# Turning P in one go: regrouped turns, copies and output projection in a fused attention and feed-forward kernel

## The chip, the cores and the metric

One core of a Trainium2 chip runs the whole program. The metric is the device time of one execution in microseconds. The engines are TensorE (PE, with PEld for its weight loads), VectorE (DVE), ScalarE (ACT), GpSimd (POOL) and SyncE (SP), which issues the transfers. Each runs its own queue in the order written and waits on semaphores.

## The reference

The input is 8 sequences of 256 tokens with 128 features. A first, small attention block of 8 heads comes ahead of the part that matters here. Then come 6 layers (DEPTH), each of them applied to the 8 sequences:

```python
def attn_layer(x, Wqkv, qs, ksc, Wo):          # 16 heads of 64, windows of 32 tokens
    q, k, v = split(x @ Wqkv, 3)
    q, k = l2norm(q) * qs, l2norm(k) * ksc     # then rotary tables on both
    out = local_attention(q, k, v)             # 32 queries see 64 keys (own and former window), softmax
    return out @ Wo                            # 1024 -> 128

def ffn_layer(x, g, bln, W1, b1, W2, b2):
    xn = (x - mean(x)) / sqrt(var(x) + 1e-05) * g + bln
    a, gate = split(xn @ W1 + b1, 2)           # 2 x 341
    return a * gelu(gate, approximate=False) @ W2 + b2

for i in range(DEPTH):
    x = attn_layer(shift_tokens(x), ...) + x
    x = ffn_layer(shift_tokens(x), ...) + x
```

## The kernel before

The 6 layers times 8 sequences are 48 units, numbered g (a "pair" in the code, since each has two halves of 128 tokens, m = 0 and 1; n = 2 * pair + m counts the halves). There is one pass, called slot, for each. Every engine has a function of the name slot(g) in its own queue, which lists the steps in an order written out by hand; all are tied by semaphores only. The slots 0 to 2 are written out, 3 to 46 are a hardware loop on TensorE and VectorE, and slot 47 is written out again. The pass works on four things at once: the attention of sequence g; the projections of q, k and v for g + 1; the output projection, residual and norm of g - 1; and the feed-forward part of f = g - 3 (LAG is 3).

A half of the attention goes like this. TensorE computes the scores of the 16 heads in two groups (g = 0 and 1 in those functions, a count of heads here, not of the pass). VectorE takes the maximum and subtracts it (centre, L1370 and L1374), into s_sb. ScalarE applies the exponential in place (exps, L1060). TensorE turns the probabilities P by transposes of 64x128 blocks into PSUM banks 4 and 5 (turn_p, which uses turn, L684), ScalarE copies them to p_t (copy_p, L1066), and TensorE multiplies them with V (attend, L766). VectorE normalises the result (L1382, L1385), TensorE turns it (turn_o), ScalarE copies it to o_t (copy_o, L1075), and in the next pass project_out (L788) multiplies it with wo_sb into bank 0.

In turn_p the first group of 8 transposes waits for both centrings and for its exponential. The second group waits for its own exponential and for the first copy, because both groups use the same places of banks 4 and 5. In between TensorE has other work: in the first half of a pass the second half of project_out(g - 1), in the second half of a pass the down projection of the feed-forward part (down, L834).

The order of the steps around this, in the first half of the pass on TensorE: scores, q of g + 1, gates_up (L806 to L808), project_out part 0, k of g + 1 (L671 to L675), turn_p 0, project_out part 1, turn_p 1, values_up (L806 to L808), attend, turn_k and turn_q, v, turn_o. In the second half: scores, q, k, turn_p 0, down, turn_p 1, mean (L795), attend, turn_k and turn_q of g + 1, variance (L801), v, turn_o.

These waits matter. The k step waits for the first gate activation (bank 7). values_up waits for all three gate activations, and its third tile, which goes to bank 0, waits for att_done (L826):

```python
up(ps[:, 1, 0:N], 0, 0)
up(ps[:, 1, N:2 * N], 0, 1).then_inc(s["f_value_up"], 1)
pe.wait_ge(s["att_done"], CREDIT + (f + LAG ...))
up(ps[:, 0, 0:N], 0, 2).then_inc(s["f_value_up"], 1)
```

att_done is given by VectorE's residual (L1393), which waits for project_out. On VectorE the first half of a pass is centre 0 and 1, the rotation products for q (L1345, L1349) and for k (L1345, L1349, which wait for k of g + 1), residual, products of the feed-forward part (L1411), normalise 0 and 1, norms (L1359). The second half has the same with add (L1418) and subtract_mean (L1400) ahead of normalise. The variance on TensorE waits for all four normalisations of the pass, since it uses bank 2.

ScalarE runs in the first half: gates (a table load at L1104, three activations at L1111, a table load back at L1113), exps 0, copy_p 0, exps 1, high (the rounding of the next input, L1011 and L1012), copy_p 1, the squares of q and k (L1019), and then the copies of k, q, o and v. In one pass of each layer a weight of the next layer is rounded here (L939), and in another one twice in the second half. The gates wait for the layer's biases.

Of the kernel before, what the change touches and what calls it, by code (L numbers as in the profile page):

```python
# [35 lines left out]
H, D = 16, 64  # L36
INNER = H * D
W = 32
SPAN = 64
# [25 lines left out]
def build(nc, xT, w1s, w2s, w3T, woT, cT, wmod, wqkv, scales, wo, params, w1, w2, consts, out):  # L65
    with ExitStack() as ctx:
# [198 lines left out]
        def layer_of(f):  # L265
            return f >> 3
# [255 lines left out]
        def _(pe):  # L522
# [155 lines left out]
            def turn(bank, c, src):  # L678


                width = src.shape[1]
                for t in range(2):
                    r = slice(64 * t, 64 * t + 64)
                    mm = pe.transpose(ps[0:width, bank + t, 64 * c:64 * c + 64], src[r], ident[r, r],  # L684
                                      tile_position=(64 * t, 0))
                return mm
# [48 lines left out]
                                           tile_position=(D * c, W * w))  # L735
                mm.then_inc(s["scored"], 1)

            def turn_p(pair, m, g):
                n = 2 * pair + m
                if g == 0:  # L740
                    pe.wait_ge(s["centred"], CREDIT + 2 * n + 2)
                else:
                    pe.wait_ge(s["p_copied"], CREDIT + 2 * n + 1)
                pe.wait_ge(s["exped"], CREDIT + 2 * n + g + 1)
                pe.sem_inc(s["pe_waited"], 1)
                for hh in range(4):
                    mm = turn(4, hh, s_sb[:, g, 2 * hh:2 * hh + 2, :].rearrange("p c k -> p (c k)"))
                mm.then_inc(s["p_turned"], 1)

            def attend(pair, m, g, over_q=True):  # L750

                n = 2 * pair + m
                if g == 0:
                    pe.wait_ge(s["v_moved"], CREDIT + 16 * (18 * pair + 8 + 10 * m))
                    pe.wait_ge(s["p_copied"], CREDIT + 2 * n + 2)
                    pe.sem_inc(s["pe_waited"], 1)
                elif over_q:
                    pe.wait_ge(s["roped"], CREDIT + 4 * n + 10)
                    pe.wait_ge(s["squared"], CREDIT + 2 * n + 5)
                    pe.sem_inc(s["pe_waited"], 1)  # L760
                for hh in range(4):
                    for w in range(4):
                        for c in range(2):
                            r = slice(D * c, D * c + D)
                            h = 4 * g + hh
                            mm = pe.matmul(ps[W * w:W * w + W, 4 - 2 * g + c, ON * hh:ON * hh + ON],  # L766
                                           p_t[r, h, W * w:W * w + W], v_sb[r, m, w, VD * h:VD * h + ON],
                                           start=True, stop=True, skip_group_check=True,
                                           tile_position=(D * c, W * w))
                mm.then_inc(s["attended"], 1)  # L770
# [6 lines left out]
                    mm = turn(2, c, o_n[:, P * c:P * c + P])  # L777
                mm.then_inc(s["o_turned"], 1)

            def project_out(pair, half):  # L780

                if half == 0:
                    pe.wait_ge(s["o_copied"], CREDIT + 2 * pair + 2)
                    pe.wait_ge(s["w_a_loaded"], 16 * layer_of(pair) + 16)
                    pe.wait_ge(s["centred"], CREDIT + 4 * pair + 5 if not isinstance(pair, int) or pair < SLOTS - 1
                               else CREDIT + 4 * pair + 4)
                for c in range(4 * half, 4 * half + 4):
                    mm = pe.matmul(ps[:, 0, 0:N], wo_sb[:, c, :], o_t[:, c, :], start=(c == 0),  # L788
                                   stop=(c == H // 2 - 1), skip_group_check=True)
                if half:  # L790
                    mm.then_inc(s["projected"], 1)

            def mean(f):
                pe.wait_ge(s["f_shifted"], CREDIT + 2 * f + 2)
# [43 lines left out]
            def slot(g, out=True, ff=True, ahead=True):  # L838
                scores(g, 0, 0)
                scores(g, 0, 1)  # L840
                if ahead:
                    q(g + 1, 0)
                if ff:
                    gates_up(g - LAG)
                if out:
                    project_out(g - 1, 0)
                if ahead:
                    k(g + 1, 0, gates=ff)
                turn_p(g, 0, 0)
                if out:  # L850
                    project_out(g - 1, 1)
                turn_p(g, 0, 1)
                if ff:
                    values_up(g - LAG)
                attend(g, 0, 0)
                attend(g, 0, 1, over_q=ahead)
                turn_k(g, 1)
                turn_q(g, 1)
                if ahead:
                    v(g + 1, 0)  # L860
                turn_o(g, 0)

                scores(g, 1, 0)
                scores(g, 1, 1)
                if ahead:
                    q(g + 1, 1)
                    k(g + 1, 1)
                turn_p(g, 1, 0)
                if ff:
                    down(g - LAG)  # L870
                turn_p(g, 1, 1)
                if out:
                    mean(g - 1)
                attend(g, 1, 0)
                attend(g, 1, 1, over_q=ahead)
                if ahead:
                    turn_k(g + 1, 0)
                    turn_q(g + 1, 0)
                if out:
                    variance(g - 1)  # L880
                if ahead:
                    v(g + 1, 1)
                if out:
                    pe.wait_ge(s["f_log"], CREDIT + g)
                turn_o(g, 1)
# [27 lines left out]
                slot(pe.snap(g))  # L913
            slot(SLOTS - 1, ahead=False)
            pe.wait_ge(s["f_done"], CREDIT + SLOTS - LAG)
            project_out(SLOTS - 1, 0)
            project_out(SLOTS - 1, 1)
            pe.wait_ge(s["f_centred"], CREDIT + SLOTS - 1)
            mean(SLOTS - 1)
            variance(SLOTS - 1)  # L920
# [5 lines left out]
        def _(act):  # L926
# [132 lines left out]
                v = s_sb[:, g, :, :].rearrange("p h k -> p (h k)")  # L1059
                act.activation(v, v, ACT.Exp).then_inc(s["exped"], 1)  # L1060

            def copy_p(pair, m, g):
                n = 2 * pair + m
                act.wait_ge(s["p_turned"], CREDIT + 2 * n + g + 1)
                act.wait_ge(s["attended"], CREDIT + 2 * n)
                act.activation(p_t[:, 4 * g:4 * g + 4, :].rearrange("p c (t k) -> p t c k", t=2),  # L1066
                               pair_of_banks(2)[:, :, 0:4 * SPAN].rearrange("p t (c k) -> p t c k", c=4),
                               ACT.Copy)\
                   .then_inc(s["p_copied"], 1)

            def copy_o(pair, m):
# [42 lines left out]

            def slot(g, ff=True, norm=True, out=True, ahead=True, more=True, after=None, layer=None):

                if ff:
                    gates(g - LAG)
                exps(g, 0, 0)
                if after == 7:  # L1120
                    round_weights(layer, 2)
                copy_p(g, 0, 0)
                exps(g, 0, 1)
                if ahead:
                    high(g + 1, 1)
                copy_p(g, 0, 1)
                if ahead:
                    square_of(g + 1, 0, 0)
                    square_of(g + 1, 0, 1)
                copy_k(g, 1)  # L1130
                copy_q(g, 1)
                if out:
                    shift(g - 1)
                copy_o(g, 0)
                if ahead:
                    copy_v(g + 1, 0)
                    inverse_norms(g + 1, 0)

                exps(g, 1, 0)
                if norm:  # L1140
                    round_norm(g - 2)
                if after == 6:
                    round_weights(layer, 0)
                if after == 2:
                    round_up(layer)
                copy_p(g, 1, 0)
                exps(g, 1, 1)
                if more:
                    high(g + 2, 0)
                copy_p(g, 1, 1)  # L1150
                if after == 6:
                    round_weights(layer, 1)
                if ahead:
                    square_of(g + 1, 1, 0)
                if out:
                    square(g - 1)
                if ahead:
                    square_of(g + 1, 1, 1)
                    copy_k(g + 1, 0)
                if out:  # L1160
                    inverse_deviation(g - 1)
# [50 lines left out]
        def _(dve):  # L1212
# [151 lines left out]
            def centre(pair, m, g):  # L1364
# [5 lines left out]
                dve.tensor_reduce(mx, src, AX.X, ALU.max)\  # L1370
                   .then_inc(s["maxed"], 1)
                dve.wait_ge(s["maxed"], CREDIT + 2 * n + g + 1)
                dve.wait_ge(s["p_turned"], CREDIT + 2 * n)
                dve.tensor_tensor(s_sb[:, g, :, :].rearrange("p (h a) k -> p a h k", a=2), src,  # L1374
                                  mx.unsqueeze(3).to_broadcast([P, 2, 4, SPAN]), ALU.subtract).then_inc(s["centred"], 1)

# [187 lines left out]
```

## Time and profile before

| | us |
|---|---|
| median of 3 runs | 1783.48 |
| lowest and highest | 1780.46, 1783.8 |
| the profiled execution | 1771.68 |
| its span, first to last instruction | 1769.9 |

| engine | busy us | share of the span |
|---|---|---|
| TensorE matmuls | 1633.4 | 92% |
| TensorE weight loads | 1264.3 | 71% |
| VectorE | 1340.1 | 76% |
| ScalarE | 1292.9 | 73% |
| GpSimd | 1061.1 | 60% |

The profile is of one execution. Matmuls overlap and their ends are modelled, so that starts are more to be trusted than ends. In the timeline a row gives its start, its duration, engine, line and operation, what it writes and reads, how many instructions were merged into the row, and in brackets how long the engine stood idle before it and for whom.

### The profile page before, as it was taken

How to read it: one execution, taken by the hardware profiler on the slowest of the kernel's cores; microseconds unless marked ns; L12 is line 12 of the kernel's file. 1: busy time of each engine (PE TensorE's matmuls, PEld its weight loads, DVE VectorE, ACT ScalarE, POOL GpSimd, SP SyncE). 2: the span in 40 equal slices, each digit the busy share in tenths (PEclk: the TensorE clock that was granted, in tenths of full speed). 3: DMA queues.
4: the chain of work that ended last, by engine and by line, in shares of the span. 5: the costliest groups of instructions: out<-in, count | busy, mean ns of one | idle time of the engine just before them, and what ended most of it. 6: DMA issues, size and time to landing. Idle time of an engine off the chain costs nothing.

```text
span 1769.9 us, 88661 instructions
## 1 busy us (share of the span) xinstructions
PE 1633.4 (92%) x36636; PEld 1264.3 (71%) x36636; DVE 1340.1 (76%) x1952; ACT 1292.9 (73%) x2124; POOL 1061.1 (60%) x767
## 2 busy tenths in 40 slices
PE   4898677799999999999999999999999999999985
PEld 2466455677777777777777777777777777777764
DVE  4465666688888878888887888888887878888852
ACT  3687445677877778777788777878777787777763
POOL 4000345567866767867678766668676676767630
PEclk8899889999999999999999999999999999999997
DMA  2000142222242222333222422222422222222220
GB/s 95 1 1 0 25 116 59 52 70 66 67 128 59 67 59 69 103 88 74 53 69 59 128 66 71 69 52 65 122 69 71 66 67 70 70 67 69 66 47 25
DMA packets 75302, 116.88 MB, mean 66 GB/s; under 512 B 17246, under 2 KB 26716, under 8 KB 74332
## 3 DMA queue, kind: packets, MB, share of 16 engines
q1 hardware_dynamic: 75228, 115.99, 26.4%
q8 instruction: 35, 0.57, 0.1%
q14 instruction: 39, 0.32, 0.1%
HBM read 19.04 MB, written 1.05 MB: 11 GB/s over the span
## 4 chain that ended last, share of the span: by engine, by line
PE 87%; issue 6%; ACT 4%; DVE 3%; DMA 0%; POOL 0%; ACTq 0%; SPq 0%; DVEq 0%
PE ps L684 14%; PE ps L788 10%; PE ps L671 9%; PE ps L766 9%; PE ps L731 8%; PE ps L675 7%; PE ps L674 7%; PE ps L834 4%; PE ps L724 2%; PE ps L806 2%; PE ps L808 2%; PE ps L807 2%; PE ps L801 2%; PE ps L795 2%; PE ps L582 1%
## 5 line engine op out<-in xcount | busy, mean ns | idle before, releaser
L411 POOL TENSOR_TENSOR arena<-arena,rnorm 128x1024 f32<-128x1024 f32 x192 | 361.6, 1904 | 352.3 <-ACT rnorm L1030 352.3
L402 POOL TENSOR_TENSOR arena<-arena 128x1024 f32<-128x1024 f32 x192 | 456.6, 2378 | 18.5 <-DVE arena L1349 15.1
L684 PEld LDWEIGHTS ps<-cst,arena 64*128 64x128 f32 x6144 | 224.4, 140 | 127.8 <-issue 119.0
L1345 DVE TENSOR_TENSOR arena<-ps,rope 128x1024 f32<-128x1024 f32 x192 | 234.7, 1222 | 94.9 <-issue 82.1
L684 PE MATMUL ps<-cst,arena 64*128 64x64 f32 x6144 | 276.8, 231 | 17.0 <-ACT arena L1060 9.4
L1066 ACT ACTIVATE arena<-ps 128x512 f32<-128x512 f32 x192 | 114.6, 597 | 175.5 <-PE ps L684 175.2
L1349 DVE TENSOR_TENSOR arena<-ps,rope 128x1024 f32<-128x1024 f32 x192 | 233.2, 1215 | 0.0
L674 PE MATMUL ps<-wqkv_lo,x_hi 128*128 128x512 f32 x576 | 229.2, 398 | 1.1 <-issue 1.1
L675 PE MATMUL ps<-wqkv_hi,x_hi 128*128 128x512 f32 x576 | 230.1, 399 | 0.0
L671 PE MATMUL ps<-wqkv_hi,x_lo 128*128 128x512 f32 x576 | 216.2, 457 | 14.8 <-issue 12.9
L1359 DVE TENSOR_REDUCE norm<-arena 128x16 f32<-128x1024 f32 x192 | 224.3, 1209 | 0.0
L1370 DVE TENSOR_REDUCE rmax<-ps 128x8 f32<-128x512 f32 x192 | 131.8, 686 | 109.0 <-PE ps L731 108.5
L766 PE MATMUL ps<-v_sb,arena 64*32 64x66 f32 x12288 | 166.5, 226 | 35.4 <-issue 19.3
L1019 ACT ACTIVATE arena<-ps 128x1024 f32<-128x1024 f32 x192 | 190.3, 1020 | 11.1 <-DVE arena L1349 11.1
L766 PEld LDWEIGHTS ps<-v_sb,arena 64*32 64x32 f32 x12288 | 138.2, 106 | 73.1 <-issue 62.9
L788 PE MATMUL ps<-arena,wo_sb 128*128 128x256 f32 x768 | 188.5, 389 | 1.2 <-issue 1.2
L731 PE MATMUL ps<-k_t,arena 64*32 64x64 f32 x12288 | 166.6, 224 | 8.2 <-issue 8.2
L1046 ACT ACTIVATE k_t<-ps 128x1024 f32<-128x1024 f32 x96 | 98.4, 1025 | 82.0 <-PE ps L684 79.5
L731 PEld LDWEIGHTS ps<-k_t,arena 64*32 64x32 f32 x12288 | 134.6, 105 | 32.4 <-issue 9.3
L788 PEld LDWEIGHTS ps<-arena,wo_sb 128*128 128x128 f32 x768 | 140.2, 192 | 20.4 <-issue 1.3
L1385 DVE TENSOR_TENSOR arena<-ps,rden 128x512 f32<-128x512 f32 x192 | 132.8, 692 | 14.4
L1374 DVE TENSOR_TENSOR arena<-ps,rmax 128x512 f32<-128x512 f32 x192 | 132.8, 692 | 14.4
(120 smaller groups left out, 2824.2 us busy)
## 6 DMA issues: line engine op xcount, KB each, us to landing
v_sb<-v_nat SPq DMA_DIRECT2D x576, 130.0 KB, 2.4
v_sb<-v_nat SPq DMA_DIRECT2D x192, 65.0 KB, 2.0
wqkv_sb<-wqkv SPq DMA_DIRECT2D x6, 1536.0 KB, 6.8
v_sb<-v_sb SPq DMA_DIRECT2D x96, 65.0 KB, 2.0
wo_sb<-wo SPq DMA_DIRECT2D x6, 512.0 KB, 8.4
w_sb<-w SPq DMA_DIRECT2D x6, 341.0 KB, 7.9
x<-xT SPq DMA_DIRECT2D x1, 1024.0 KB, 6.2
out<-x SPq DMA_DIRECT2D x4, 256.0 KB, 2.3
```

The source lines that it names most:

```text
L402: pool.tensor_tensor(t_cos[:, m, j, :], t_cos[:, m, j, :], t_sin[:, j, :], ALU.add)\
L411: pool.tensor_tensor(x, x, rnorm[:, H * j:H * j + H].unsqueeze(2).to_broadcast([P, H, D]), ALU.mult).then_inc(s[done], 1)
L671: pe.matmul(ps[:, bank + c, :], x_lo[:, m, :], wqkv_hi[:, w], start=True, stop=False)
L674: pe.matmul(ps[:, bank + c, :], x_hi[:, m, :], wqkv_lo[:, w], start=False, stop=False)
L675: mm = pe.matmul(ps[:, bank + c, :], x_hi[:, m, :], wqkv_hi[:, w], start=False, stop=True)
L684: mm = pe.transpose(ps[0:width, bank + t, 64 * c:64 * c + 64], src[r], ident[r, r], tile_position=(64 * t, 0))
L731: mm = pe.matmul(ps[W * w:W * w + W, 4 * g + c, SPAN * hh:SPAN * hh + SPAN], q_t[r, 4 * g + hh, W * w:W * w + W], k_t[r, 4 * g + hh, P * m ...
L766: mm = pe.matmul(ps[W * w:W * w + W, 4 - 2 * g + c, ON * hh:ON * hh + ON], p_t[r, h, W * w:W * w + W], v_sb[r, m, w, VD * h:VD * h + ON], ...
L788: mm = pe.matmul(ps[:, 0, 0:N], wo_sb[:, c, :], o_t[:, c, :], start=(c == 0), stop=(c == H // 2 - 1), skip_group_check=True)
L1345: dve.tensor_tensor(t_cos[:, m, j, :].rearrange("p (h d) -> p h d", h=H), src.rearrange("p a (h d) -> p (a h) d", h=8), tc.unsqueeze(1).to ...
L1349: dve.tensor_tensor(t_sin[:, j, :].rearrange("p (h s d) -> p h s d", h=H, s=2), src.rearrange("p a (h s d) -> p (a h) s d", h=8, s=2)[:, : ...
L1359: dve.tensor_reduce(norm2[:, H * j:H * j + H], sq[:, j, :].rearrange("p (h d) -> p h d", h=H), AX.X, ALU.add).then_inc(s["normed"], 1)
```

## The change

TensorE turns both groups of P with sixteen transposes in one go (turn_p without its group), into all eight places of banks 4 and 5. The step waits for both centrings and both exponentials, and no longer for a copy. ScalarE copies all of it with one instruction of 128x1024 in place of two of 128x512. project_out is one step with eight column blocks, placed where its first part stood. On ScalarE the gates of the pass come behind the two exponentials of the first half instead of ahead of them, and in the second half both exponentials are ahead of the copy. The semaphores p_turned and p_copied count once per half instead of twice.

```diff
-            def turn_p(pair, m, g):
+            def turn_p(pair, m):
                 n = 2 * pair + m
-                if g == 0:
-                    pe.wait_ge(s["centred"], CREDIT + 2 * n + 2)
-                else:
-                    pe.wait_ge(s["p_copied"], CREDIT + 2 * n + 1)
-                pe.wait_ge(s["exped"], CREDIT + 2 * n + g + 1)
+                pe.wait_ge(s["centred"], CREDIT + 2 * n + 2)
+                pe.wait_ge(s["exped"], CREDIT + 2 * n + 2)
                 pe.sem_inc(s["pe_waited"], 1)
-                for hh in range(4):
-                    mm = turn(4, hh, s_sb[:, g, 2 * hh:2 * hh + 2, :].rearrange("p c k -> p (c k)"))
+                for h in range(H // 2):
+                    mm = turn(4, h, s_sb[:, h // 4, 2 * (h % 4):2 * (h % 4) + 2, :].rearrange("p c k -> p (c k)"))
                 mm.then_inc(s["p_turned"], 1)
...
                 if out:
-                    project_out(g - 1, 0)
+                    project_out(g - 1)
                 if ahead:
                     k(g + 1, 0, gates=ff)
-                turn_p(g, 0, 0)
-                if out:
-                    project_out(g - 1, 1)
-                turn_p(g, 0, 1)
+                turn_p(g, 0)
                 if ff:
                     values_up(g - LAG)
...
-                turn_p(g, 1, 0)
+                turn_p(g, 1)
                 if ff:
                     down(g - LAG)
-                turn_p(g, 1, 1)
...
-            def copy_p(pair, m, g):
+            def copy_p(pair, m):
                 n = 2 * pair + m
-                act.wait_ge(s["p_turned"], CREDIT + 2 * n + g + 1)
+                act.wait_ge(s["p_turned"], CREDIT + n + 1)
                 act.wait_ge(s["attended"], CREDIT + 2 * n)
...
+                exps(g, 0, 0)
+                exps(g, 0, 1)
                 if ff:
                     gates(g - LAG)
-                exps(g, 0, 0)
                 if after == 7:
                     round_weights(layer, 2)
-                copy_p(g, 0, 0)
-                exps(g, 0, 1)
                 if ahead:
                     high(g + 1, 1)
-                copy_p(g, 0, 1)
+                copy_p(g, 0)
...
-                copy_p(g, 1, 0)
                 exps(g, 1, 1)
                 if more:
                     high(g + 2, 0)
-                copy_p(g, 1, 1)
+                copy_p(g, 1)
```

## Rows read from the trace of the kernel before

**Rows 1.** The page: busy time, share of the span and instructions by engine.
```profile
PE 1633.4 (92%) x36636; PEld 1264.3 (71%) x36636; DVE 1340.1 (76%) x1952; ACT 1292.9 (73%) x2124; POOL 1061.1 (60%) x767
```

**Rows 2.** Windows: length; busy us of PE, PEld, DVE, ACT, POOL; clock; DMA.
```profile
350.00:1690.00 1340.00, 1317.24 (x31822) 1038.01 (x31818) 1106.39 (x1557) 1056.68 (x1707) 937.88 (x677) 1.00 0.30 74
...
809.72:842.12 32.40, 30.78 (x740) 23.95 (x737) 26.42 (x37) 24.60 (x40) 22.05 (x17) 1.00 0.29 68
903.56:934.26 30.70, 30.45 (x741) 24.02 (x737) 25.59 (x37) 24.05 (x39) 20.74 (x16) 1.00 0.28 65
```

**Rows 3.** Timeline, first half of pass 21, from the end of k.
```profile
931.22 0.40 PE L675 MATMUL ps<-wqkv_hi,x_hi 128*128 128x512 f32 x1
...
931.79 1.23 DVE L1345 TENSOR_TENSOR arena<-ps,rope 128x1024 f32<-128x1024 f32 x1 [1.80 <-issue]
...
932.94 1.22 DVE L1349 TENSOR_TENSOR arena<-ps,rope 128x1024 f32<-128x1024 f32 x1
...
934.26 0.42 DVE L1393 TENSOR_TENSOR h<-ps,h 128x256 f32 x1
...
935.07 0.28 PE L806 MATMUL ps<-f_hi,w_lo 128*128 128x256 f32 x1
...
935.51 1.72 PE L766 MATMUL ps<-v_sb,arena 64*32 64x66 f32 x128
```

**Rows 4.** The chain: the two parts of the output projection; the page's group of its weight loads.
```profile
928.48 1.73 PE ps L788 x8
...
932.01 1.92 PE ps L788 x8
...
L788 PEld LDWEIGHTS ps<-arena,wo_sb 128*128 128x128 f32 x768 | 140.2, 192 | 20.4 <-issue 1.3
```

**Rows 5.** Timeline, ScalarE in pass 21, then its groups by line.
```profile
926.07 1.28 ACT L1104 ACT_TABLE_LOAD   x1
...
927.81 0.47 ACT L1111 ACTIVATE f_a<-ps,par 85x256 f32<-85x256 f32 x1 [0.45 <-PE ps L808]
...
929.38 1.28 ACT L1113 ACT_TABLE_LOAD   x1
...
930.67 0.63 ACT L1060 ACTIVATE arena<-arena 128x512 f32<-128x512 f32 x1
...
L1019 ACT ACTIVATE arena<-ps 128x1024 f32<-128x1024 f32 x172 | 170.4, 1020 | 0.0
...
L1066 ACT ACTIVATE arena<-ps 128x512 f32<-128x512 f32 x173 | 103.3, 597 | 147.2 <-PE ps L684 147.2
```

**Rows 6.** Timeline, second half of pass 20: VectorE's chain and the variance.
```profile
910.97 0.69 DVE L1370 TENSOR_REDUCE rmax<-ps 128x8 f32<-128x512 f32 x1 [0.90 <-PE ps L731]
...
917.20 1.22 DVE L1349 TENSOR_TENSOR arena<-ps,rope 128x1024 f32<-128x1024 f32 x1
...
918.03 0.72 PEld L766 LDWEIGHTS ps<-v_sb,arena 64*32 64x32 f32 x64 [0.48 <-issue]
...
918.33 0.47 DVE L1418 SCALAR_TENSOR_TENSOR h<-ps,par,h 128x256 f32 x1
...
918.72 0.41 DVE L1400 TENSOR_TENSOR f_a<-f_a,ps 128x256 f32<-128x256 f32 x1
...
920.22 0.69 DVE L1385 TENSOR_TENSOR arena<-ps,rden 128x512 f32<-128x512 f32 x1
...
920.96 0.70 PE L801 MATMUL ps<-f_a,cst 128*128 128x256 f32 x2
```

**Rows 7.** Timeline: waits in the passes around a change of layer.
```profile
836.65 0.74 PE L671 MATMUL ps<-wqkv_hi,x_lo 128*128 128x512 f32 x2 [0.27 <-ACT f_a L1111]
...
839.41 0.46 PE L684 MATMUL ps<-cst,arena 64*128 64x64 f32 x8 [1.08 <-ACT arena L1060]
...
950.80 0.85 PE L766 MATMUL ps<-v_sb,arena 64*32 64x66 f32 x64 [1.19 <-ACT arena L1019]
```

**Rows 8.** Timeline: the turn of P in the last pass.
```profile
1705.14 0.46 PE L684 MATMUL ps<-cst,arena 64*128 64x64 f32 x8 [1.19 <-issue]
```

More of the change, by code:

```diff
@@ L754, in attend @@
                     pe.wait_ge(s["v_moved"], CREDIT + 16 * (18 * pair + 8 + 10 * m))
-                    pe.wait_ge(s["p_copied"], CREDIT + 2 * n + 2)
+                    pe.wait_ge(s["p_copied"], CREDIT + n + 1)
                     pe.sem_inc(s["pe_waited"], 1)
@@ L778, in turn_o, with project_out @@
                 mm.then_inc(s["o_turned"], 1)
[L780 to L787, printed above, removed]
+            def project_out(pair):
+                pe.wait_ge(s["o_copied"], CREDIT + 2 * pair + 2)
+                pe.wait_ge(s["w_a_loaded"], 16 * layer_of(pair) + 16)
+                pe.wait_ge(s["centred"], CREDIT + 4 * pair + 5 if not isinstance(pair, int) or pair < SLOTS - 1
+                           else CREDIT + 4 * pair + 4)
+                for c in range(H // 2):
                     mm = pe.matmul(ps[:, 0, 0:N], wo_sb[:, c, :], o_t[:, c, :], start=(c == 0),
                                    stop=(c == H // 2 - 1), skip_group_check=True)
-                if half:
-                    mm.then_inc(s["projected"], 1)
+                mm.then_inc(s["projected"], 1)
             def mean(f):
@@ L915, in _ @@
             pe.wait_ge(s["f_done"], CREDIT + SLOTS - LAG)
-            project_out(SLOTS - 1, 0)
-            project_out(SLOTS - 1, 1)
+            project_out(SLOTS - 1)
             pe.wait_ge(s["f_centred"], CREDIT + SLOTS - 1)
@@ L1060, in exps @@
                 act.activation(v, v, ACT.Exp).then_inc(s["exped"], 1)
-            def copy_p(pair, m, g):
+            def copy_p(pair, m):
                 n = 2 * pair + m
-                act.wait_ge(s["p_turned"], CREDIT + 2 * n + g + 1)
+                act.wait_ge(s["p_turned"], CREDIT + n + 1)
                 act.wait_ge(s["attended"], CREDIT + 2 * n)
-                act.activation(p_t[:, 4 * g:4 * g + 4, :].rearrange("p c (t k) -> p t c k", t=2),
-                               pair_of_banks(2)[:, :, 0:4 * SPAN].rearrange("p t (c k) -> p t c k", c=4),
-                               ACT.Copy)\
+                act.activation(p_t.rearrange("p c (t k) -> p t c k", t=2),
+                               pair_of_banks(2).rearrange("p t (c k) -> p t c k", c=8), ACT.Copy)\
                    .then_inc(s["p_copied"], 1)
@@ L1372, in centre @@
                 dve.wait_ge(s["maxed"], CREDIT + 2 * n + g + 1)
-                dve.wait_ge(s["p_turned"], CREDIT + 2 * n)
+                dve.wait_ge(s["p_turned"], CREDIT + n)
                 dve.tensor_tensor(s_sb[:, g, :, :].rearrange("p (h a) k -> p a h k", a=2), src,
```

## The prediction

> **What bounds the kernel now.** I read the page first [rows 1]: TensorE is busy for 92% of the span, the next engine for 76%. By windows [rows 2] the 1340 us of the looped part have TensorE busy for 98% at a granted clock of 1.00, while VectorE has 83% and ScalarE 79%. A steady pass of the loop is 30.70 us long and TensorE is busy 30.45 us of it. So the order of TensorE's own queue sets the time, nothing on TensorE becomes cheaper or dearer unless a wait appears or goes, and a wait that appears there cannot be absorbed by slack. Then I read one pass in order of time, first half [rows 3] and second half [rows 6].
>
> First half [rows 3]. The last product of k for the next sequence starts at 931.22. VectorE has waited for it 1.80 us and starts the two products of k's rotation at 931.79 and 932.94; behind them in its queue stands the residual, 934.26 to 934.68, which releases the third tile of the values (PE L806 at 935.07), and then the attention (935.51). Between k and the values TensorE does eight turns of P, the second part of the output projection (932.01 [rows 4]) and eight more turns. That projection fills the time in which VectorE is at k's rotation. The third tile comes 0.39 us after the residual has ended, so this is nearly critical already.
>
> Second half [rows 6]. VectorE goes through from the first maximum at 910.97 to the last normalisation, which ends at 920.91, with its work one behind the other. The variance on TensorE waits for that normalisation and starts at 920.96. In all 44 looped passes I found it 0.05 to 0.10 us behind. So two chains of the same length, TensorE's and VectorE's, end there together.
>
> **The output projection in one piece** moves its second half ahead of k. By the chain of waits its eight instructions took 1.73 us in the first half and 1.92 us in the second, where the switch to the turns is in it [rows 4]; I take 1.74 for the shift of k. k's gate wait costs nothing (below). So in pass 21 the last product of k goes from 931.22 to 932.96 and VectorE's k rotation from 931.79 to 933.53. Its second instruction follows 1.15 later (932.94 minus 931.79), at 934.68. The residual follows that at 1.13, the spacing of two such neighbours where nothing is waited for (917.20 to 918.33 [rows 6]): 935.81. In the kernel before it was 1.32 (932.94 to 934.26), since it had also to wait for the projection, which is now long done. It takes 0.42: it ends at 936.23, and with the 0.05 to 0.15 that a release takes the third tile starts at 936.3. It was 935.07: **1.25 us later in each pass**. TensorE has nothing to fill this: k ends at 933.2, the sixteen turns in one go take 0.7 to 0.8, the first two tiles of the values 0.8, so that it stands from 934.8 to 936.3. The turns themselves cost the same sixteen instructions; only one switch is saved, and it is saved in a stretch that now ends in a wait. After the third tile the first half goes on as before: the attention comes at 936.75, the second half's scores 1.25 us later. Bounds: 1.54 for the shift (eight weight loads at 192 ns, were the matmuls wholly behind them [rows 4]) and the quickest release give 1.0; 1.92, no gain of 0.19 at the residual and 0.15 for the release give 1.7.
>
> **One copy of P in place of two.** Two copies of 0.60 go, one of 1.02 comes [rows 5]: 0.18 us of ScalarE, which is not the bound. In the first half the copy starts at about 934.2 and ends at 935.3, before the values' third tile: hidden behind the new wait. Were that wait not there, the attention could start at 935.4, as now. In the second half the attention waited for the second copy (0.48 us at 918.03 [rows 6]). Now all of P is turned ahead of the down projection, and the copy runs beside that and the mean. So that wait goes and the attention starts some 0.5 us sooner. But VectorE's chain is not shortened by it: the add and the mean's subtraction stand at 918.33 and 918.72 whatever TensorE does, the normalisations follow, and the variance stays at 920.96 [rows 6]. TensorE only waits there instead. Worth between 0 and 0.5 us a pass; I take 0, because VectorE's row is unbroken.
>
> **The gates behind the exponentials.** Before, the table load starts at 926.07, the gates run to the load back at 929.38, and the exponential has to wait until 930.67 [rows 5]. After, both exponentials are over at 928.2, load 1.28, the first gate (0.47) done at 930.0, the other two by the same row at 930.9, the second load at 932.2. k, at 931.6, needs the first gate; the values, at 934.0, need all; both are met. Cost 0. This leaves ScalarE free by 932.8 with the next rounding done, ahead of the copy.
> On this step a rule speaks against the change. The rows show the load back at 929.38, 1.28 us long, and the exponential at 930.67, with 0.01 us between [rows 5]. The Trainium skill, "ScalarE: Activation LUTs", section "What ACT_TABLE_LOAD costs", puts a drain of about 1380 ns beside each load, some 2.66 us together. By that the gates behind the exponentials would push the copy of P behind the turns to 936.5 in a usual pass, still just under the new wait, but in the 5 passes that also round a weight there it would come about 0.8 us too late: an estimate of +4 us on the sum. The trace doesn't show that drain, so the sum goes by the row.
>
> **Waits that go.** In 4 passes, the first that use a layer's new biases, the gates come late: k waits 0.27 us for them and the turn 1.08 for the exponential behind them [rows 7]; such a pass takes 32.40 in place of 30.70, the other three 32.3 [rows 2], so 1.6 each. With the exponentials first and k later, both go: −6.4. In 5 passes two weight roundings sit between ScalarE's steps and the second attention waits for a square (1.19 us at 950.80 [rows 7]). Now a rounding stands before the second exponential (turns +0.5 later) and the chain copy, rounding, square ends about 0.5 sooner than before: −2.5. Bounds 0 and 1.1 each. In the last pass the turn waited 1.19 for the late exponential [rows 8] and no k lies there: about −1.5. What the first three passes, unrolled and with no or little feed-forward work, gain or lose I can't price from these rows; I take 0, bounds ±3.
>
> **The sum.** 44 passes have both a k ahead and a feed-forward part: 44 × 1.25 = 55.0; 55.0 − 6.4 − 2.5 − 1.5 = 44.6. The profiled execution took 1771.7 us (span 1769.9), so it would be 1816. The median of the runs shown is 11.8 us above the profiled one, which no row explains; I add the difference to the median: 1783.5 + 44.6 = 1828. Ends: 44 × 1.0 less 13 is +31; 44 × 1.7 less 8 is +67.
>
> **Rivals.**
> - *The new wait comes and VectorE's chain gives something back* (chance 0.12). If in the second half TensorE's chain really is the later one and VectorE could follow it, 0.5 × 44 = 22 goes off: 1806. For it: VectorE stands idle 0.90 us before 910.97, and the variance's start shows no idle time. Against: that idle time lies before scores that TensorE itself gives, and the 0.05 us in all passes.
> - *The wait doesn't decide* (chance 0.06): if the values' third tile could start when TensorE arrives, as when k's rotation is quicker or the residual's release isn't what it waits for, only what goes is left: 44 × 0.5 + 10 = 32 less, 1752. It decides if the shift of k is below 0.5 us; the eight instructions would have to take a third of what they show. The other side of the forecast.
> - *The clock falls in the new gap* (chance 0.03). TensorE's level was 1.00 throughout, also where it stood 1.08 us in a pass [rows 2, 7], so a gap of 1.5 us should not do it. If one microsecond in each pass ran at 1.2 GHz instead of 2.4, it would be 44 × 0.5 to 1 more: about 1860.
> - *It does not do what it says*: excluded by the queues, which run in the order written; the three moves are all there in the diff.
>
> **How the numbers follow.** The forecast has 0.79. Its own ends are +31 and +67; the 1806 case and a few microseconds of uncertainty of the median widen the lower end: 1808 to 1851. A change of up to 0.2% (3.6 us) is about what a measurement of this kernel cannot tell from none. Faster holds the 1752 case and a little of the mixed ones: 0.07; within 0.2% 0.02; slower 0.91.
>
> **What would show it.** VectorE's residual starts 1.13 us behind the second k product instead of 1.32; TensorE stands about 1.5 us ahead of the values' third tile (L806) in each pass with VectorE's residual as releaser; k's rotation starts 1.7 us later; pass length 31.95 in place of 30.70; the second half keeps its 13.8 us with the attention earlier and the variance 0.05 to 0.1 behind the last normalisation; the passes of 32.3 us are gone. Wrong would be: a pass of 30.7 or less, a wait ahead of the attention with a copy or square as releaser, or a second half shorter by 0.4.

## The result, and the profile after

| | before | after |
|---|---|---|
| median of 4 runs each | 1781.97 us | 1800.28 us |
| lowest and highest | 1776.37, 1783.8 | 1797.86, 1808.43 |
| profiled execution, its span | 1771.68, 1769.9 | 1798.79, 1797.0 |

The changed kernel is slower: ratio 1.0116, 95% interval 1.0075 to 1.0157. Timed again later beside the kernel before it was 1.0157 (1.0124 to 1.0190; 1805.41 against 1779.63 us). The forecast was slower, with 1828 us and a range of 1808 to 1851; the time lies below the range.

First the page's busy line and the clock's line of the changed kernel, to set beside [rows 1].

```profile
PE 1624.4 (90%) x36636; PEld 1273.5 (71%) x36636; DVE 1342.3 (75%) x1952; ACT 1283.2 (71%) x2028; POOL 1062.0 (59%) x767
...
PEclk8899889999999999999999999999999999999997
```

TensorE executes the same 36636 matmuls and is busy about as long; its share fell, so it stands longer. A pass is seen in the windows view (columns as in [rows 2]). This is pass 21: 31.85 us against 30.70, TensorE busy 30.29.

```profile
899.23:931.08 31.85, 30.29 (x740) 24.23 (x737) 25.55 (x37) 23.83 (x37) 20.48 (x16) 1.00 0.26 63
```

Where it stands is in the timeline of the first half of pass 21, to be read against [rows 3].

```profile
908.54 0.40 PE L675 MATMUL ps<-wqkv_hi,x_hi 128*128 128x512 f32 x1
...
908.87 0.71 PE L684 MATMUL ps<-cst,arena 64*128 64x64 f32 x16
909.11 1.23 DVE L1333 TENSOR_TENSOR arena<-ps,rope 128x1024 f32<-128x1024 f32 x1 [3.52 <-issue]
...
909.70 1.02 ACT L1057 ACTIVATE arena<-ps 128x1024 f32<-128x1024 f32 x1 [1.38 <-PE ps L684]
...
910.26 1.21 DVE L1337 TENSOR_TENSOR arena<-ps,rope 128x1024 f32<-128x1024 f32 x1
...
911.39 0.41 DVE L1381 TENSOR_TENSOR h<-ps,h 128x256 f32 x1
...
911.86 0.39 PE L802 MATMUL ps<-f_hi,w_lo 128*128 128x256 f32 x1 [1.37 <-DVE h L1381]
...
912.40 1.72 PE L764 MATMUL ps<-v_sb,arena 64*32 64x66 f32 x128
```

VectorE now stands 3.52 us for k, not 1.80. The two products of k's rotation are 1.15 apart, the residual (now L1381) follows at 1.13, and the third tile of the values (L802) has stood 1.37 us when the residual is over. The waits view of the looped part says that this is so in 42 passes, and that beside it only the variance (L797) waits for VectorE:

```profile
PEld ps L802 <- DVE h L1381: 66.2, 42, 1.6
...
PE ps L802 <- DVE h L1381: 57.6, 42, 1.4
...
PEld ps L797 <- DVE arena L1373: 6.3, 36, 0.2
```

The second half of the same pass, against [rows 6]:

```profile
918.55 0.69 DVE L1358 TENSOR_REDUCE rmax<-ps 128x8 f32<-128x512 f32 x1 [0.99 <-PE ps L731]
...
925.09 1.72 PE L764 MATMUL ps<-v_sb,arena 64*32 64x66 f32 x128
...
925.87 0.47 DVE L1406 SCALAR_TENSOR_TENSOR h<-ps,par,h 128x256 f32 x1
...
927.67 0.69 DVE L1373 TENSOR_TENSOR arena<-ps,rden 128x512 f32<-128x512 f32 x1
...
928.41 0.70 PE L797 MATMUL ps<-f_a,cst 128*128 128x256 f32 x2
```

The attention starts 6.54 us behind the first maximum; it was 7.06 (918.03 less 910.97), some 0.5 more. The last normalisation ends 9.81 behind it (9.94 before), and the variance follows by 0.05 as before.

From here on passes are measured from the first matmul of the mask (L724) of one half to that of the next.

| part of the span | before | after | difference | forecast |
|---|---|---|---|---|
| up to pass 0 | 219.6 | 219.5 | −0.1 | 0 |
| passes 0 to 2 | 112.1 | 99.4 | −12.7 | 0 |
| first halves of passes 3 to 46 | 752.5 | 807.5 | +54.9 | +48.6 |
| their second halves | 613.3 | 604.4 | −8.8 | −2.5 |
| pass 47 to the end | 72.4 | 66.1 | −6.2 | −1.5 |
| sum | 1769.9 | 1797.0 | +27.1 | +44.6 |

The loop gave +46.1 and the forecast for it was +46.1. That they are equal is luck: the first halves came out 6.3 us above the forecast, the second halves 6.3 below it. Of the 6.3 us in the first halves 3.1 are three passes in which TensorE's clock fell (below) and 1.7 are pass 3, the first one of the loop. What failed is the two edges, the passes ahead of the loop and the one behind it.

### The profile page after: what moved, and what is told of

Same layout as the page of the kernel before. It is cut to its first block, busy times and chain, and to the rows that moved or that the text cites. A ratio compares the mean times of both kernels' runs of the same rounds, so it can differ in the third digit from the quotient of the medians.

```text
span 1797.0 us, 88257 instructions
## 1 busy us (share of the span) xinstructions
PE 1624.4 (90%) x36636; PEld 1273.5 (71%) x36636; DVE 1342.3 (75%) x1952; ACT 1283.2 (71%) x2028; POOL 1062.0 (59%) x767
## 4 chain that ended last, share of the span: by engine, by line
PE 70%; issue 17%; DVE 8%; ACT 3%; DVEq 1%; DMA 0%; POOL 0%; ACTq 0%; SPq 0%
PE ps L684 11%; PE ps L731 8%; PE ps L671 8%; PE ps L764 8%; PE ps L675 6%; PE ps L674 6%; PE ps L785 5%; DVE arena L1337 3%; PE ps L724 2%; PE ps L802 2%; DVE arena L1333 2%; PE ps L797 2%; PE ps L830 2%; PE ps L804 1%; PE ps L803 1%
## 5 line engine op out<-in xcount | busy, mean ns | idle before, releaser
L684 PEld LDWEIGHTS ps<-cst,arena 64*128 64x128 f32 x6144 | 220.5, 139 | 100.1 <-issue 90.6
L684 PE MATMUL ps<-cst,arena 64*128 64x64 f32 x6144 | 262.8, 228 | 14.3 <-POOL arena L411 2.6
L1010 ACT ACTIVATE arena<-ps 128x1024 f32<-128x1024 f32 x192 | 190.6, 1018 | 12.6 <-DVE arena L1337 12.6
L785 PE MATMUL ps<-arena,wo_sb 128*128 128x256 f32 x768 | 175.6, 382 | 1.2 <-issue 1.2
L1051 ACT ACTIVATE arena<-arena 128x512 f32<-128x512 f32 x192 | 120.1, 628 | 72.4 <-DVE arena L1362 61.6
L1057 ACT ACTIVATE arena<-ps 128x1024 f32<-128x1024 f32 x96 | 98.3, 1024 | 94.8 <-PE ps L684 94.7
L785 PEld LDWEIGHTS ps<-arena,wo_sb 128*128 128x128 f32 x768 | 144.0, 192 | 19.6 <-issue 1.3
L802 PE MATMUL ps<-f_hi,w_lo 128*128 128x256 f32 x288 | 92.8, 322 | 64.9 <-DVE h L1381 60.3
```

## The experiments

Each stood beside the kernel before on the same chip. The table gives, from each profile, the usual half passes, passes 0 to 2 together, the first half of pass 47, where pass 0 begins, and the measured ratio with its interval.

| kernel | first half | second | passes 0–2 | 47, first | pass 0 at | ratio to before |
|---|---|---|---|---|---|---|
| before | 16.92 | 13.78 | 112.1 | 18.55 | 219.6 | |
| before, second profile | 16.91 | 13.79 | 110.1 | 17.80 | 222.8 | |
| changed | 18.19 | 13.66 | 99.4 | 13.73 | 219.5 | 1.0116 (1.0075–1.0157) |
| changed, second profile | 18.20 | 13.66 | 98.7 | 14.06 | 220.0 | 1.0157 (1.0124–1.0190) |
| one piece only | 18.22 | 13.76 | 113.5 | 17.86 | 226.0 | 1.0296 (1.0253–1.0339) |
| gates only | 17.07 | 13.77 | 114.3 | 16.10 | 226.3 | 1.0020 (0.9997–1.0043) |
| turn and copy only | 17.35 | 13.66 | 96.4 | 17.07 | 226.5 | 0.9942 (0.9911–0.9972) |
| changed, residual first | 17.28 | 13.67 | 101.2 | 14.06 | 226.5 | 0.9892 (0.9865–0.9919) |
| changed, split behind the turns | 17.07 | 13.67 | 94.9 | 13.88 | 219.3 | 0.9871 (0.9834–0.9908) |
| split, gates between | 16.93 | 13.66 | 98.6 | 15.73 | 227.3 | 0.9891 (0.9857–0.9924) |
| split, variance in v | 17.07 | 13.98 | 103.5 | 14.05 | 226.3 | 0.9952 (0.9914–0.9991) |
| that, and q's copy first | 17.09 | 13.56 | 96.5 | 13.72 | 226.5 | a single run |
| split, all edits | 16.93 | 13.55 | 94.2 | 17.41 | 220.1 | 0.9857 (0.9820–0.9893) |

**The residual ahead of k's rotation.**

```diff
                 if ahead:
                     rope_products(g + 1, 0, 0)
-                    rope_products(g + 1, 0, 1)
                 if out:
                     residual(g - 1)
+                if ahead:
+                    rope_products(g + 1, 0, 1)
```

> The changed kernel with one swap on VectorE: in the first half of a pass the residual stands ahead of k's two rotation products instead of behind them. Theory A (the values' third tile waits for k's rotation plus residual): the residual now runs while VectorE would idle for k, the wait of 1.37 us ahead of the third tile goes, the first half of a pass falls from 18.18 to about 16.9 us (the attention is then held by the copy of P or by TensorE's own work), the pass to about 30.5, and the span by some 44 x 1.3 = 57 us, to about 1740; that is also below the kernel before. Rival B (TensorE lost the time to something else that came with the one-piece projection, such as the order of its own instructions): the first half stays at 18.0 or more. Rival C (another wait of like size takes its place, the copy of P or the squares on ScalarE): the first half falls by less than 0.6 us and the attention shows a wait on ScalarE.

The wait at the third tile is gone and the median is 1761.05 us, below the kernel before but not the expected 1740. The first half fell by 0.91, not by 1.3. The wait that came in its place is the turn of k, which waits for the last feed-forward product, since VectorE does k's rotation ahead of those:

```profile
930.56 0.43 DVE L1381 TENSOR_TENSOR h<-ps,h 128x256 f32 x1 [2.26 <-PE ps L785]
...
935.61 1.44 PE L684 MATMUL ps<-cst,arena 64*128 64x64 f32 x32 [0.27 <-DVE f_a L1399]
```

So A holds for 0.91 of the 1.3 us. What is left of it is another wait, as C had it in kind, but at the turn of k, for VectorE, and small (10.9 us over 39 passes).

**The second part of the projection behind the turns.**

```diff
                 if out:
-                    project_out(g - 1)
+                    project_out(g - 1, 0)
                 if ahead:
                     k(g + 1, 0, gates=ff)
                 turn_p(g, 0)
+                if out:
+                    project_out(g - 1, 1)
```

> The changed kernel with the output projection in two parts again: the first where the whole now stands, the second behind the sixteen turns of P. Theory A: k is back at its old time, the second part covers VectorE's rotation of k, the first half of a pass falls to 16.8 to 16.95 us, the second stays at 13.66, so the pass is about 30.5 and the span some 58 us below the changed kernel, about 1740. Rival B (the sixteen turns in one go or the copy in one instruction cost the time): the first half stays at 18.0.

Median 1754.42. The place of these four column blocks alone is worth 1.1 us in each first half, and rival B is out. It fell short of 16.95 by a wait of k for the gates, which the late k of the changed kernel had hidden:

```profile
PEld ps L671 <- ACT f_a L1106: 18.5, 43, 2.0
```

**Only the projection in one piece**, all else as before:

```diff
                     project_out(g - 1, 0)
+                    project_out(g - 1, 1)
                 if ahead:
                     k(g + 1, 0, gates=ff)
                 turn_p(g, 0, 0)
-                if out:
-                    project_out(g - 1, 1)
                 turn_p(g, 0, 1)
```

> The kernel before with only one part of the change: both parts of the output projection stand ahead of k; P is still turned in two groups with two copies, the gates still come first. Theory A: the first half of a pass rises from 16.91 to about 18.2 us, as in the changed kernel, since the second copy (ready at about 936 in the time of pass 21) is hidden behind the wait for the residual (936.3); the second half stays at 13.78; so about +55 us on the span, some 1825. Rival B (turning and copying in one go is what costs): the first half stays below 17.2. Rival D (without the single copy the turns' wait for the first copy adds to it): the first half is above 18.6.

18.22 and 13.76 us, median 1833.46: this part alone costs more than the whole change (+53 us against the same runs of before). The halves are theory A's, but TensorE does not stand where A has it. It stands at the second turns, for the second exponential (L1059), which on ScalarE is behind the first copy, and that is behind the first turns and so behind the late k. The waits view, and the place in pass 21 (L1392 is the residual, the last line the third tile):

```profile
PE ps L684 <- ACT arena L1059: 55.6, 42, 1.3
...
937.34 0.46 PE L684 MATMUL ps<-cst,arena 64*128 64x64 f32 x8 [1.33 <-ACT arena L1059]
...
938.06 0.42 DVE L1392 TENSOR_TENSOR h<-ps,h 128x256 f32 x1
...
938.54 0.38 PE L806 MATMUL ps<-f_hi,w_lo 128*128 128x256 f32 x1
```

The third tile comes 0.06 us behind the end of the residual and shows no wait of its own. So with two turns the late k lengthens two chains, over ScalarE and over VectorE, and they end together. This kernel shows what the late k costs. That in the changed kernel it is the residual's chain is shown by its waits view and by the two experiments above.

**Only the gates moved** (the two exponentials, then the gates, then the first copy):

```diff
-                if ff:
-                    gates(g - LAG)
                 exps(g, 0, 0)
+                exps(g, 0, 1)
+                if ff:
+                    gates(g - LAG)
                 if after == 7:
                     round_weights(layer, 2)
                 copy_p(g, 0, 0)
-                exps(g, 0, 1)
```

> The kernel before with only the gates moved: on ScalarE both exponentials of the first half come first, then the gates with their table loads, then the two copies of P. Theory A: an ordinary pass stays at 30.70 within 0.15 us, and the four passes of 32.3 to 32.4 us, where late biases held the exponential back, lose about 1.1 to 1.6 each: the span falls by some 5 us, to about 1765. Rival E (a drain of more than a microsecond beside each table load, not seen as idle time, now reaches the copy of P): an ordinary pass rises by 0.5 us or more, over 20 us in all.

Median 1782.46, no gain, where 1765 was expected. An ordinary pass rose by 0.15 us, not by the 0.5 or more of rival E. With k at its old place it waits 0.45 us for the gate (18.8 us over 42 passes at the weight loads), of which 0.15 reach the pass; and a late pass takes 32.6 to 32.7, not less, for k then waits for the late gate. The gain that the forecast gave to the gates' move needs the late k.

**Only turn and copy in one** (the split kernel above, with the gates ahead of both exponentials):

```diff
-                exps(g, 0, 0)
-                exps(g, 0, 1)
                 if ff:
                     gates(g - LAG)
+                exps(g, 0, 0)
+                exps(g, 0, 1)
```

> The kernel before with one part of the change alone: P is turned in one go and copied in one instruction; the output projection keeps its second part between the turns and the values, and the gates stay ahead of both exponentials. Theory F (the first passes and the last, which have no other work between the turns, gained from the single turn and copy): passes 0 to 2 together take 95 to 101 us, as in the changed kernel (99.4), and not 112 to 114 as in the kernels with two turns and two copies; the first half of pass 47 falls to about 16. Rival G (the start differs from kernel to kernel by chance or by the place of code): 108 us or more. In the loop the turns have to wait for the second exponential, which now stands behind the gates (over at 931.9 in the time of pass 21, against 931.5 for the turns): first half 16.9 to 17.3, second 13.66. Span about 1745.

Passes 0 to 2 took 96.4 us: theory F. In the loop the turns wait for the second exponential and the first half is 17.35 us, just above what was expected. The first half of pass 47 took 17.07 us, not about 16, and the span was 1768.2, not 1745. The kernel is 0.6% faster than the one before.

**The gates between the exponentials**, on the split kernel:

```diff
                 exps(g, 0, 0)
-                exps(g, 0, 1)
                 if ff:
                     gates(g - LAG)
+                exps(g, 0, 1)
```

> The changed kernel with the output projection split as before (second part behind the sixteen turns) and with the gates between the two exponentials instead of behind both. In the split version k waited 0.43 us in each pass for the gates' activation (L671 behind L1106, 43 times). Theory H: the gate comes 1.3 us earlier, k's wait goes, the second exponential (over at about 931.4) is still in time for the turns at 931.5, and the first half of a pass falls from 17.07 to 16.75 to 16.9; some 8 to 12 us on the span against the split version (1743.6 at the same start). Rival: the turns now wait for the second exponential by as much, and the first half stays at 17.0 or more.

The first half is 16.93 us, k's wait is left in 4 passes only. But those passes became longer (32.8 to 33.1 us), and the median, 1757.05, doesn't differ from the split kernel's beyond the intervals.

**The variance inside v**, on the split kernel:

```diff
-                if out:
-                    variance(g - 1)
                 if ahead:
-                    v(g + 1, 1)
+                    v(g + 1, 1, (lambda: variance(g - 1)) if out else None)
+                elif out:
+                    variance(g - 1)
```

> The changed kernel with the split output projection, and with the variance's two matmuls moved from ahead of v into v, behind v's first two matmuls (0.46 us later in the queue). Theory I (in the second half of a pass the variance waits for VectorE's last normalisation, which took back most of what the attention gained): the wait of 0.17 us and the slowed turns ahead of it go, the second half falls from 13.67 to 13.3 to 13.5, 7 to 16 us in all. Rival J (TensorE's own work bounds the second half): it stays at 13.62 or more. The first half stays at 17.07.

The second half rose to 13.98. The wait for the normalisation is gone, and the next scores wait for the copy of q, which stands behind the variance's logarithm on ScalarE:

```profile
928.57 0.30 PE L726 MATMUL ps<-mask_bf,ident_bf 64*64 64x256 bf16 x4 [0.37 <-ACT arena L1035]
```

So this one told nothing of I and J. **The same with q's copy ahead of the logarithm:**

```diff
-                if out:
-                    inverse_deviation(g - 1)
                 if ahead:
                     copy_q(g + 1, 0)
+                if out:
+                    inverse_deviation(g - 1)
```

> As the kernel with the variance inside v, and on ScalarE the copy of q stands ahead of the variance's logarithm, since there the next scores waited 0.37 us for that copy (second half 13.97 us). Theory I (VectorE's last normalisation held the variance and so the second half): with both waits gone the second half falls from 13.67 (split version) to 13.3 to 13.5. Rival J (TensorE's own work bounds it): 13.6 to 13.7; the wait for the normalisation then cost nothing that can be had back. First half 17.07, passes 0 to 2 in 95 to 104 us.

13.56: 0.11 less than 13.67, between J's range and I's. Once the new copy was in, VectorE's chain held the second half by 0.1 us only.

**All edits together**, on the split kernel with the gates between:

```diff
-                exps(g, 0, 1)
                 if ff:
                     gates(g - LAG)
+                exps(g, 0, 1)
...
+                    v(g + 1, 1, (lambda: variance(g - 1)) if out else None)
...
+                if ahead:
+                    copy_q(g + 1, 0)
                 if out:
                     inverse_deviation(g - 1)
```

> The version that should beat both: one turn and one copy of P, the output projection's second part behind the turns, the gates between the two exponentials, the variance inside v and the copy of q ahead of its logarithm. Theory I: a pass of 16.93 + 13.4 = 30.3 us, the span 10 to 12 us below the version without the last two edits (which took 30.59 a pass), so about 1745 at a start of 227 us. Rival J: a pass of 30.6 and no difference to it.

Median 1752.49, ratio 0.9857: below both kernels. A pass is 30.48 us in place of 30.59, nearer to rival J's 30.6 than to theory I's 30.3; against the split kernel alone (0.9871) it is no measurable gain.

**The two kernels unchanged.**

> The kernel before, unchanged, for a second profile. Theory K (the program before pass 0 has two levels, 219.5 and 226.5 us, whatever the kernel, which is most of the 11.8 us between the first profile of this kernel and its median): pass 0 begins at one of the two; the looped passes are again 30.70 with halves of 16.92 and 13.78; passes 0 to 2 take 110 to 116 us. Theory F wants these last numbers too; rival G would have them scatter down to 100.

> The changed kernel, unchanged, timed again beside the kernel before and profiled again. Theory K and F together: looped passes again 31.86 us (18.18 and 13.66), passes 0 to 2 again 95 to 104 us, pass 0 beginning anywhere between 219 and 228 us. The difference of the medians is then +1.0% to +1.5%, 18 to 27 us: 46 from the loop less about 13 from the first passes and 6 from the last. Rival G (the first passes' gain was chance): passes 0 to 2 take 108 or more and the difference is +30 us or more.

The halves came out as before to 0.02 us, passes 0 to 2 to 2.0 and 0.7 us: theory F, and rival G is out. The ratio, 1.0157, is just above the expected 1.0% to 1.5%. Theory K is wrong: where pass 0 begins is no matter of two levels, for besides 219.3 to 220.1 and 226.0 to 227.3 us there is 222.8. That part of the program is the same in all thirteen profiles.

## Why the prediction was wrong

**The new wait: right, in place and size.** The third tile waits for the residual, and the usual first half grew by 1.27 us (forecast 1.25). Moving its second part back alone removes 1.1 of it, and giving the residual its turn earlier removes 0.9. Moving only the projection costs as much (1.30), there by a wait of the same length at the second turns. The residual's own steps came out as 1.15, 1.13 and 0.41, the idle time 1.37 where some 1.5 stood.

**The clock: a rival at 0.03 that came true in a small part.** In 3 of 44 passes (6, 28 and 30) the granted clock fell to half 0.3 us after TensorE had gone on behind that gap. Pass 28, in windows of 2 us and more:

```profile
1130.00:1134.00 4.00, 3.96 (x33) 3.03 (x31) 1.40 (x2) 2.57 (x4) 2.92 (x4) 1.00 0.29 68
1134.00:1136.00 2.00, 0.66 (x3) 0.55 (x3) 2.00 (x4) 2.00 (x3) 0.96 (x1) 0.89 0.00 0
1136.00:1138.00 2.00, 2.00 (x125) 1.80 (x128) 1.16 (x4) 0.04 (x1) 1.40 (x1) 0.50 0.00 0
1138.00:1140.00 2.00, 2.00 (x60) 1.75 (x46) 1.83 (x4) 0.58 (x1) 0.00 (x0) 0.76 0.00 0
```

The granted clock (the first figure behind the five busy times) goes 1.00, 0.89, 0.50, 0.76. Each such pass is 1.0 us longer. The second profile of the changed kernel has 5 and the one-piece kernel 4. In passes 4 to 46 of the other ten profiles, the two of the kernel before among them, there is none. Pass 3 is a case of its own. In its first half TensorE stands once for 1.3 to 2.2 us in every profile, and in 10 of the 13, one of the kernel before among them, the clock fell in that stop or within 1.6 us of its end. The forecast had the clock at 1.00 throughout; its windows began at 350 us, behind pass 3.

**The copy in one and VectorE's chain: right in kind, mis-sized in the small.** The attention came some 0.5 us sooner, VectorE's chain took nearly all back, 0.12 a pass was left where I took 0 (13.78 against 13.66). The 5 passes with two roundings lost 0.87 each in their second half; the forecast had 0.5. Together −8.8 against −2.5.

**The gates: right.** k and the values did not wait for them (but for 0.1 to 0.3 us of k in three of the late passes), and the late passes lost about 1.5 of their 1.6 us (first halves of 18.2 to 18.4, where 18.5 to 18.6 and 1.3 more were due). The experiments add that this rests on the late k. On the drain beside a table load (the Trainium skill, "ScalarE: Activation LUTs", "What ACT_TABLE_LOAD costs"): the trace doesn't agree with 1380 ns. Each of the 96 loads takes 1.28 us, and in the kernel with the residual first the load begins 0.02 us behind the exponential and the gate 0.02 behind the load:

```profile
925.92 0.63 ACT L1051 ACTIVATE arena<-arena 128x512 f32<-128x512 f32 x1 [0.69 <-DVE arena L1362]
...
926.57 1.28 ACT L1094 ACT_TABLE_LOAD   x1
...
927.87 1.19 ACT L1101 ACTIVATE f_a<-ps,par 85x256 f32<-85x256 f32 x3
```

**The step that failed: the edges.** "What the first three passes, unrolled and with no or little feed-forward work, gain or lose I can't price from these rows; I take 0, bounds ±3." They gained 12.7 us, and the last pass with the tail 6.2 where I had 1.5: together 17.4 us, and the sum was off by 17.5. The four profiles with two turns and two copies have 110.1 to 114.3 us in passes 0 to 2, the nine with one 94.2 to 103.5, whatever else differs. The price could in part have been read. In the loop there is other work between the two turns. In these passes there is little, so the chain lay open: turns, copy, exponential, turns, copy. The second exponential stands behind the first copy on ScalarE, and the second turns wait for it. The timeline of the kernel before, second half of pass 0:

```profile
247.55 0.46 PE L684 MATMUL ps<-cst,arena 64*128 64x64 f32 x8
...
248.06 0.60 ACT L1066 ACTIVATE arena<-ps 128x512 f32<-128x512 f32 x1 [2.33 <-PE ps L684]
...
249.27 0.46 PE L684 MATMUL ps<-cst,arena 64*128 64x64 f32 x8 [1.26 <-ACT arena L1060]
...
250.47 1.72 PE L766 MATMUL ps<-v_sb,arena 64*32 64x66 f32 x105 [0.73 <-issue]
```

and the same place in the changed kernel:

```profile
244.62 0.71 PE L684 MATMUL ps<-cst,arena 64*128 64x64 f32 x16
...
246.50 1.59 PE L764 MATMUL ps<-v_sb,arena 64*32 64x66 f32 x106 [1.17 <-issue]
```

From the first turn to the attention 2.92 us became 1.88. That is 1.04 in each of the four halves that have nothing of weight between the turns, or 4.2 us. In the kernel with only the gates moved, whose first halves have both exponentials ahead of the copy, the first half of pass 0 shows 2.44, so that about half of the 1.04 is the exponential's place ahead of the copy and the rest the single turn and copy. In the first halves of passes 1 and 2 the projection's second part lay between the turns, and what the turns saved went to its new place ahead of k: the attention of pass 1 started 10.28 us into the pass before and 10.37 after (9.33 with the second part behind the turns). The windows of passes 0 to 2, before and after:

```profile
219.57:331.71 112.14, 83.48 (x2118) 64.31 (x2117) 71.64 (x95) 58.04 (x95) 61.27 (x42) 0.90 0.31 79
```

```profile
219.49:318.93 99.44, 80.57 (x2118) 62.88 (x2118) 71.27 (x95) 57.55 (x89) 59.41 (x41) 0.92 0.35 89
```

TensorE's busy time is 2.9 us less at a clock of 0.92 against 0.90, and its idle time 9.8 us less (28.7 against 18.9). Most of that idle time are stops in the middle of a group of equal matmuls, with no semaphore between them, which occur in the unrolled passes in every kernel. This one cuts the attention of the half shown above in two; below it is the row of the DMA view for passes 0 to 2 (packets, MB, share).

```profile
253.79 0.66 PE L766 MATMUL ps<-v_sb,arena 64*32 64x66 f32 x23 [1.60 <-issue]
...
q8 instruction: 17, 0.28, 1.1%
```

Counted over 0.3 us each, there are 9 such stops in passes 0 to 2 of the kernel before, 19.1 us, and 7 after, 12.3 us (in the second profiles 18.0 and 12.9). So they are 6.8 of the 12.7 us. They go with queue q8, whose packets the profile names "instruction": each of the 114 stops of this size in passes 0 to 4 of all thirteen profiles ends 2.2 to 3.2 us behind the start of such a packet, where a moment taken at random does so in some 14% of cases. Passes 5 to 46 have neither packets of q8 nor stops. So they look like waits for code that is run for the first time. Both kernels have 17 of these packets in passes 0 to 2. Why the stops are shorter after the change is open. The kernels with two turns have 17.1 to 19.1 us of them there and the others 10.8 to 17.4, so this part of the gain goes with the single turn, but that the turn is its cause is not shown.

The last pass is written out too. The 1.19 us for the late exponential went, as forecast. What I had left out is here, too, mostly the stops: two of 1.86 and 2.32 us in its attention before, none after (1.86 and 1.45 against 1.57 in the second profiles). The place of the gates counts as well: its first half takes 13.7 to 14.1 us where one turn goes with the gates behind both exponentials, and 15.7 to 17.4 where the gates stand earlier.

**The offset.** I added 11.8 us between the first profile and the median of before to both sides. That was a property of one execution: the kernel's second profile was 1775.73 us, and the profile of the changed kernel lay 1.5 below its median. This made some 10 us of the 28 by which 1828 was too high. From the two profiles alone the change costs 27 us, from the medians 18 in the first set and 26 in the second. The range shared the error, and its lower end of 1808 lay even above the 1806 of its own first rival.

## What to carry to other kernels

Work between two waits of one engine may be the cover of a chain on another: before it is moved, follow what runs beside it to the last thing that waits for that. A loop's price times its count is only a part of a forecast. The first and last passes lack the cover that the loop has, and each chain that is hidden in the loop has to be priced there openly. Edits that cost and edits that pay can be in one change: here one turn and one copy with the gates behind the exponentials won, the projection's move lost twice that, and keeping the first without the second gave 0.987 of the time before. And a version that gives the expected number may do it by another wait: look where the engine stands before the number is taken as proof.

## What I had not expected of the hardware

A stop of 1.37 us on TensorE was followed by half the clock in 3 and 5 of 44 passes (4 with the one-piece kernel's stop of 1.33 us), and in none of passes 4 to 46 of the ten profiles whose kernels lack such a stop. TensorE also stood for 11 to 19 us in three passes of unrolled code, inside runs of equal matmuls, and each such stop ended 2.2 to 3.2 us behind a packet of the queue named "instruction". And the same code ahead of pass 0 took from 219.3 to 227.3 us in different executions, more than many of the differences under study.
